# Where the gather engine stops in each stage of a graph network: one group of edges later

## The reference

```
xn = layernorm(x)
x = x + gnn(xn, edges) + mixer(xn)        # layer 0: a graph convolution, a hyperbolic linear-attention mixer
x = x + experts(layernorm(x))             # 8 gated experts, 2 per node
xn = layernorm(x)
x = x + gnn1(xn, edges) + transformer(xn) # layer 1: linear attention and a feed-forward block
x = x + experts1(layernorm(x))            # 16 experts, 2 per node
```

```
layer 0: agg_h = segment_sum(xn_scaled[src], dst);  agg_e = segment_sum(edge_feat, dst)
layer 1: neighbour = segment_sum(edge_weight[:, None] * xn[src], dst)
```

## Time and profile before

| what | us |
|---|---|
| median of 3 executions (2255.16 to 2262.03) | 2258.12 |
| the profiled execution | 2264.34 |
| span of the profiled execution | 2262.6 |
| Pool busy over the span (47%) | 1068.4 |
| of that the 784 indirect DMAs of L575 | 790.5 |
| Pool idle just before those, in steps of "issue" | 233.7 |
| TensorE busy over the span (84%) | 1907.8 |

### The profile page before, as it was taken

How to read it: one execution, slowest core, us unless ns; L and a number is a source line. 1 busy time by engine, 2 the same in 40 slices (tenths; PEclk the granted TensorE clock), 3 DMA queues, 4 the chain that set the end, 5 groups by cost and what they waited for, 6 DMA issues and landing times. The chain is left out here.

```text
span 2262.6 us, 33217 instructions
## 1 busy us (share of the span) xinstructions
PE 1907.8 (84%) x10298; PEld 1561.5 (69%) x10299; DVE 1248.4 (55%) x3125; ACT 603.2 (27%) x1303; POOL 1068.4 (47%) x1063
## 2 busy tenths in 40 slices
PE   6599788888576899999984989799999766799976
PEld 4366566666363799999982667578877653688865
DVE  7533687777475444444448568525544386233446
ACT  0222343333342111111113211122222132233324
POOL 0576777777520222222220667777777200355532
PEclk9999899999886899999996999899999987899998
DMA  7554555555364011011005533434444408212224
GB/s 228 152 147 130 151 145 144 141 140 148 88 274 170 28 35 34 30 35 34 30 22 165 177 102 113 115 116 131 124 127 116 138 1 355 80 63 65 67 62 145
DMA packets 175992, 258.49 MB, mean 114 GB/s; under 512 B 74113, under 2 KB 139357, under 8 KB 173460
## 3 DMA queue, kind: packets, MB, share of 16 engines
q0 software_dynamic: 49344, 131.89, 20.2%
q1 hardware_dynamic: 114644, 113.45, 15.2%
q10 hardware_dynamic: 11904, 11.96, 1.6%
HBM read 203.27 MB, written 56.86 MB: 115 GB/s over the span
## 5 line engine op out<-in xcount | busy, mean ns | idle before, releaser
L575 POOL DMA_INDIRECT agg_message<-table,edges_src x784 | 790.5, 1008 | 397.7 <-issue 233.7
L630 PE MATMUL agg_partial<-agg_message,moe_up 128*128 128x321 f32 x784 | 243.3, 465 | 71.2 <-DMA agg_message<-table,edges_src 58.6
L2463 PEld LDWEIGHTS ex_p_h<-ex_xT,ex_own_up 128*128 128x128 f32 (+1 forms) x2464 | 280.0, 191 | 2.8 <-issue 1.4
L2463 PE MATMUL ex_p_h<-ex_xT,ex_own_up 128*128 128x128 f32 (+1 forms) x2464 | 280.7, 276 | 1.0 <-DVE ex_xT L2514 1.0
L630 PEld LDWEIGHTS agg_partial<-agg_message,moe_up 128*128 128x128 f32 x784 | 158.5, 205 | 147.5 <-issue 86.0
L630 PE MATMUL agg_partial<-agg_message,agg_onehot 128*128 128x256 f32 x784 | 188.4, 394 | 19.4 <-DMA agg_message<-table,edges_src 10.4
L2422 POOL DMA_INDIRECT ex_x<-moe_in,route_token_at x58 | 57.3, 987 | 309.8 <-PE ex_p_x L2453 240.7
L2518 DVE COPY ex_own_up<-moe_up 128x1280 f32 x114 | 100.7, 884 | 167.2 <-PE ex_p_h L2463 166.4
L630 PEld LDWEIGHTS agg_partial<-agg_message,agg_onehot 128*128 128x128 f32 x784 | 153.6, 198 | 48.4 <-issue 25.1
L640 ACT COPY agg_span<-agg_partial 128x321 f32<-128x321 f32 (+1 forms) x112 | 44.9, 401 | 435.4 <-PE agg_partial L633 426.5
L2588 POOL DMA_INDIRECT ex_x<-moe_in,route_token_at x66 | 64.4, 975 | 172.9 <-PE ex_p_x L2619 93.1
(11 more groups left out here) (588 smaller groups left out, 3318.3 us busy)
## 6 DMA issues: line engine op xcount, KB each, us to landing
agg_message<-table,edges_src POOLq DMA_INDIRECT x784, 2.8
agg_message<-in_edge_rows SPq DMA_DIRECT2D x56, 224.0 KB, 4.3
moe_up<-in_f_w SPq DMA_DIRECT2D x8, 1386.0 KB, 21.7
sums<-agg_span SPq DMA_DIRECT2D x56, 160.5 KB
moe_up<-in_f_w SPq DMA_DIRECT2D x4, 2048.0 KB
moe_down<-in_f_w SPq DMA_DIRECT2D x4, 2048.0 KB, 32.7
sums<-agg_span SPq DMA_DIRECT2D x56, 128.0 KB
moe0b_down<-in_f_w SPq DMA_DIRECT2D x8, 768.0 KB, 10.5
```

Source lines behind the costliest of these rows:

```text
L575: pool.indirect_dma_start(out=to[:, k * w:k * w + D], out_offset=None, in_=self.table, in_offset=bass.IndirectOffsetOnAxis(ap=self.edges.s ...
L630: mm = pe.matmul(to, hot[:, k * P:(k + 1) * P], msg[:, k * w:(k + 1) * w], start=(k == 0), stop=(g == 0 and k == GE - 1))
L2463: return pe.matmul(to, own_up[:, o:o + n], xT[:, k * D + c * P:k * D + (c + 1) * P], start=(c == 0), stop=(c == 1))
```

## The change

A constant AHEAD = 2 takes the place of the one group by which Pool ran beyond the stage's products. The list of prepare (group 0) stays, and so does everything on the other engines, the sizes of the rings and the waits.

```
+AHEAD = 2
 qkv_channels:
-            for g in range(groups[0] + 1, groups[-1] + 2):
+            for g in range(groups[0] + 1, groups[-1] + AHEAD + 1):
 mixer:
-            for g in range(groups[0] + 1, EG):
+            for g in range(groups[0] + AHEAD, EG):
 keys_and_values:
-            for e in range(0, groups[-1] + 2):
+            for e in range(0, groups[-1] + AHEAD + 1):
 attend:
-            for e in range(groups[0] + 1, groups[-1] + 2):
+            for e in range(groups[0] + AHEAD, groups[-1] + AHEAD + 1):
 feed_forward:
-            for e in range(groups[0] + 1, EG):
+            for e in range(groups[0] + AHEAD, EG):
```

## The result

Timed side by side, the kernel before took 2258.62 us (2255.16 to 2262.03, 6 runs) and the changed one 2245.11 us (2242.42 to 2248.12, 6 runs): a ratio of 0.9935 (0.9925 to 0.9946). In a second comparison it was 0.9927 (0.9906 to 0.9948). So the change gains 13.5 and 17.9 us by the medians, and 0.65 and 0.73% by the ratios; the two intervals overlap. The forecast was 2238.8, within 2231 to 2250.

A forecast was written before the change was run, and what follows sets the result against it. Pool's gather schedule was taken to set the end of layer 0, and TensorE to bound most of layer 1. Savings of 8.3 us (layer 0) and 11.0 (layer 1) sum to 19.3, taking 2258.12 to 2238.8, range 2231 to 2250.

The forecast's parts named there:

- the hold-up: End of layer 0: DVE's row of 25 operations holds one gather of group 55 for 6.42 us; taken as staying.
- End of qkv_channels: Layer 0's first barrier: group 16 gathered ahead of it is covered by SP's last issue, cost 0, otherwise 0 to 1.2 us.
- TensorE in the mixer: Layer 0: products 16 start behind ACT's copy, 6.9 us earlier, plus 0 to 1.8 us for a higher clock.
- The ring: Layer 0, mixer: Pool waits for group 21's slot, loses 1.3 to 0 us, and is then 7.9 to 9.2 us early.
- End of keys_and_values: Layer 1: group 6 overfills Pool's hole at the barrier, so all other engines enter attend 2.9 us late.
- Attend: no wait at group 13: Layer 1: gather 13 keeps 1.3 us in hand and doesn't wait for its slot; the stage ends 1.9 us early.
- rival 2: Layer 1 gives only its barrier, 1.9 us, as something else holds TensorE or attend's 1.3 us are used up: 2247.9; chance 0.12.
- Feed_forward: Layer 1: products 21 no longer wait for rows, so the transposes start 8.4 to 11.0 us early, taken as 10.4.
- bad case: End of layer 0: the first of four gathers begun in DVE's row is caught; the three behind it add 3.8 us.
- Rival 3: Barriers wait for Pool and rows fetched ahead save TensorE nothing: 4.1 us slower, 2262.2; chance 0.04.
- rival 4: No change: layer 0 gives 2.9 us and layer 1 only its barrier's 1.9, 2253.3 or within 0.3%; chance 0.07.
- Rival 1: End of layer 0: DVE's lock on gathers falls otherwise, none caught 2234.6, the first caught 2242.6; chance 0.13.

The follow-up runs named there:

- second comparison: The changed kernel once more, no edit, against the kernel before on the same chip: 2242.76 us (6 runs), ratio 0.9927; profiled a second time, span 2239.8.
- the two boundaries alone: Two kernels, layer 0 as changed; in layer 1 only group 6 moved ahead of its barrier (2250.91 us, ratio 0.9965), or only group 21 (2249.76 us, 0.9951).
- rows A: Rows of 25 SCALAR_TENSOR_TENSOR operations on VectorE beside Pool's gathers; eight were run in a kernel of its own, one execution, 552.34 us.
- Rows D: Eight rows of 25 TENSOR_TENSOR operations with two SBUF inputs beside Pool's gathers, in the same kernel of its own, 552.34 us.

## Why the prediction was right, and where its terms were off

1. **The sum.** The saving was 18.9 us of span between the two executions with a held gather and 17.6 between the two without, for a forecast of 19.3 from an execution with one. The timed medians moved by 13.5 and 17.9, so the forecast took about 1.5 to 6 us too much; each single profile also moves by 1 to 3 us in code that nobody changed ("between" goes from 637.0 to 638.9, "rest" from 478.3 to 481.4). The 2245.0 forecast for the profiled execution, against 2245.45, is luck in so far as both executions happened to have the hold-up. Terms too large are 8.3, for which 7.4 came, and 11.0, for which 10.0 came. One bound of the recorded sum doesn't follow from its own terms: with attend only 0.6 us early and the slow pace, products 21 would give 7.1 us and not 8.0 as the low end of layer 1.

2. **End of qkv_channels: cost nothing.** Right: gathers over at 228.8, SP's last issue done at 228.87 + 0.36 = 229.2.

3. **TensorE in the mixer: 6.9 to 8.7 us.** It gained 6.4. The next late thing was ACT's copy, as forecast. The 0 to 1.8 us more for a higher clock came out at 0: a wait of 3.49 us was left where the forecast had about two, and the clock over products 16 was 0.70, no better than the 0.69 of the earlier trace rows. The wait was longer because products 15 took 4.03 us here, and 5.71 in the execution from which the forecast was worked, while ACT's copy came no sooner.

4. **The ring: 1.3 to 0 us.** Layer 0's mis-sized step. In the pair of executions with the hold-up TensorE ended products 18 only 5.9 us earlier, so the slot of group 21 came free later than worked out, and Pool's 9.2 us of lead shrank to 6.6 at group 21 and to 5.9 at group 22, under the forecast's 7.9. In the pair without it, Pool's 8.9 us shrank to 7.6. Behind this the lead drifted with the length of single gathers, up to 8.9 us at the end of the one pair's group 55 and down to 6.5 in the other. So layer 0 gave 9.0 us in the one pair and 7.2 in the other, and one pair alone can't tell the term to better than 1 or 2 us. Over the executions without a hold-up it is 7.4: four kernels with the change in layer 0 end it at 603.0 in the mean (601.8 to 603.6), two without the change at 610.4.

5. **End of keys_and_values: 2.9 us late.** Too small. Pool did pass the barrier as forecast (1306.74, which is 63.1 us into the layer; 1315.0 was 62.7). But TensorE is 5.9 us late (5.1 in the second execution): its wait is 4.66 - 1.36 = 3.3 us longer, and the clock was at its lower level for more than half of the queries behind it, which cost 7.09 - 4.55 = 2.5 us more. The forecast knew this effect from the earlier trace rows and did not apply it to a wait that the change itself adds.

6. **Attend: no wait at group 13.** Wrong for the same cause. The slots came free 3 us later than worked out, the 1.3 us left over were gone, and Pool waited 2.34 - 0.30 = 2.0 us. The prediction had named this as a sign of being wrong, a wait for a slot in attend of more than 1 us, and it came. That is rival 2's mechanism, in a small dose. The stage was left with Pool last, as forecast, yet only 0.7 us early (203.2 to 202.5) instead of 1.9.

7. **Feed_forward: 8.4 to 11.0 us.** 9.1 by the transposes, and 10.0 at the end of layer 1. The mechanism is shown by the two boundaries alone: without Pool's lead, products 21 wait 6.89 us.

8. **The hold-up.** In three of nine profiles: one of three without the change in layer 0, two of six with it. It costs 4.8 us in the kernel before (615.2 to 610.4, forecast 4.2) and 3.2 with the change (606.15 to 603.0). It comes in some executions of either kernel, so it was right to leave it in the sum. How many of the timed runs had it no profile shows: this stays open, and so does whether it is why the gains by the two comparisons' medians differ by some 4 us, which the overlapping intervals allow to be nothing. The forecast's bad case, in which the first of four gathers is caught, didn't occur: in all seventeen rows A (nine profiles and the eight rows alone) gathers begun up to 3.3 us into the row passed in at most 1.3 us, and all eleven that began 4.0 to 4.8 us into it waited for its end.

Rival 3 fell: the barriers did wait for Pool, by more than the 2.9 us, but the rows fetched ahead were handed on and paid for it. Rival 2 fell because layer 1 gave 10.0 us and not 1.9, and rival 4 by the timings. Rival 1 said that the change would shift the hold-up; it comes and goes in both kernels, and with it in both or in neither the saving is 18.9 and 17.6.

## What to carry to other kernels

Work fetched ahead of a barrier pays only if the engine that waits for it isn't the same one that the barrier now holds: follow the lead through every later stage, for one boundary can fetch it and another spend it, and each alone looks worthless. Price a wait that a change adds by its length and by the slow clock behind it, and read the latter from a row of the same work behind such a wait. And before trusting a sum against one profiled execution, look for an operation of odd length in it (6.42 us among 0.95 us) and profile the same kernel twice.

## What the runs showed of the hardware

**A row of SCALAR_TENSOR_TENSOR holds a gather.** SCALAR_TENSOR_TENSOR of 128x256 in a row of 25 (9.98 us) held the one indirect gather that began 4.0 to 4.8 us in until 0.8 us after the row, eleven times in eleven. TENSOR_TENSOR in a row of 8.47 us held none, with the gathers at 1.03 to 1.14 us beside it instead of 0.95. What lets the ones before it pass, and which trait of the operation holds it, was not tried. The Trainium skill (SBUF — State Buffer, Who interferes with whom) tells of a lock between VectorE's operations on two SBUF inputs and GpSimd's reads, and infers for tensor_tensor that it doesn't stall descriptor generation. Rows D agree, with no gather held. Rows A, whose operation also has two SBUF inputs, show that the inference doesn't extend to them.

**A short wait can nearly halve the pace.** Behind waits of TensorE of 3.47 to 5.40 us at a barrier the same work took up to 1.8 times as long: products 20 5.5 to 5.8 us instead of 3.3 (behind 3.47 and 3.48 us), the queries 6.4 to 7.3 us instead of 4.55 (behind 4.14 to 5.40 us). The longer wait didn't cost more: the queries took 7.30 us behind 4.14 us and 6.44 behind 5.40, and products 20 took 4.88 us behind 8.94. Behind 1.36 us the queries kept 4.55 us at a granted clock of 1.00. Behind 1.65 us they took 6.24 us, with the clock at 0.50 from 1302.7 to 1304.7, and in both executions TensorE had been busy without a break for the 10 us before. So the length of the wait alone doesn't tell it.
